# The last layer norm of an attention and expert layer begun two tiles early: rows of the last two tiles summed on chip and written over

## The reference

```python
logits = xf @ wr + br
topk_vals, topk_idx = jax.lax.top_k(logits, K)          # K = 2 of E = 4 experts
gates = jax.nn.softmax(topk_vals, axis=-1)
h = gelu(einsum('nd,edh->enh', xf, w1) + b1)            # 256 -> 1024
y = einsum('enh,ehd->end', h, w2) + b2                  # 1024 -> 256
...
out = einsum('nk,nkd->nd', gates, y_sel - c_sel + c_sum)
x = layernorm(x + out)                                  # 4096 tokens (8 x 512), 256 features
```

## Time and profile before

| | us |
|---|---|
| median of 3 runs | 1062.55 (1061.18 to 1064.93) |
| the profiled execution | 1066.83 |
| its span on the core | 1065.1 |
| PE busy | 929.2 (87%) |
| DVE busy | 835.0 (78%) |
| ACT busy | 495.6 (47%) |
| POOL busy | 430.5 (40%) |

### The profile page before, as it was taken

The page is one execution under the profiler, slowest core; times in us unless marked ns, Lnnn a source line. Parts: engine busy times, 40 slices in busy tenths (PEclk is TensorE's granted clock), DMA queues, the critical chain, the costliest instruction groups (busy, mean ns, idle before and its releaser), DMA issues.

```text
span 1065.1 us, 26698 instructions
## 1 busy us (share of the span) xinstructions
PE 929.2 (87%) x8002; PEld 676.0 (63%) x8003; DVE 835.0 (78%) x2990; ACT 495.6 (47%) x1045; POOL 430.5 (40%) x376
## 2 busy tenths in 40 slices
PE   3688999997989989998896799899999999999920
PEld 1244656555656566565664577788889778988920
DVE  4637789797898988988987789887777887777737
ACT  3256554553555635555355545343444333333304
POOL 6418055383453653735537512223222442322321
PEclk8789999999999999999999989999999999999975
DMA  4785103224133032230133432223223332232356
GB/s 141 250 213 147 32 22 105 80 70 118 35 91 92 25 120 59 62 119 2 51 111 120 159 110 41 41 52 47 46 42 61 81 59 45 50 50 50 50 124 222
DMA packets 61535, 90.33 MB, mean 85 GB/s; under 512 B 8620, under 2 KB 51136, under 8 KB 60384
## 3 DMA queue, kind: packets, MB, share of 16 engines
q1 hardware_dynamic: 45832, 62.73, 19.9%
q0 software_dynamic: 14304, 21.90, 11.2%
q10 hardware_dynamic: 1280, 4.19, 1.1%
HBM read 52.80 MB, written 35.86 MB: 83 GB/s over the span
## 4 chain that ended last, share of the span: by engine, by line
PE 55%; DVE 25%; issue 6%; DMA 6%; SPq 4%; ACT 2%; DVEq 1%; POOL 0%; ACTq 0%; POOLq 0%
PE sm L1375 6%; PE st L1375 5%; PE ms L1160 5%; PE sm L1388 5%; PE pv L1388 5%; PE sm L1242 5%; PE st L1202 4%; PE pv L1222 4%; DVE junk L1780 4%; PE ms L1300 3%; DVE arena_b L1942 3%; DVE arena_b L1940 2%; PE ms L1272 2%; DVE beaten L1727 2%; PE st L1204 2%
## 5 line engine op out<-in xcount | busy, mean ns | idle before, releaser
L1780 DVE CUSTOM_DVE_ANT_0 junk<-sm,mask_ts 128x512 bf16<-128x512 f32 (+3 forms) x512 | 220.1, 485 | 61.1 <-PE sm L1242 58.7
L900 POOL DMA_INDIRECT sums<-arena_b x70 | 112.6, 1609 | 294.7 <-DVE arena_b L1968 280.6
L1028 ACT ACTIVATE arena_b<-st 128x512 f32<-128x512 f32 x320 | 180.2, 598 | 101.6 <-PE st L1204 100.2
L1202 PE MATMUL st<-arena_a 128*128 128x384 f16 (+3 forms) x512 | 126.5, 304 | 24.1 <-ACT arena_b L1028 16.7
L1242 PE MATMUL sm<-arena_a 128*128 128x512 f16 (+3 forms) x512 | 112.9, 309 | 18.0 <-DVE maxes L1780 11.9
L1942 DVE TENSOR_TENSOR arena_b<-arena_b 128x256 f16<-128x256 f32 x280 | 120.2, 429 | 9.6
L1099 ACT ACTIVATE arena_b<-sm,arena_b 128x256 f32<-128x256 f32 x140 | 66.1, 474 | 125.5 <-PE sm L1375 107.0
L1375 PE MATMUL st<-arena_b,arena_a 128*128 128x256 f16 x840 | 115.6, 275 | 7.7 <-DVE arena_b L1659 6.9
L1940 DVE CAST arena_b<-arena_b 128x256 f16<-128x256 f32 x280 | 88.8, 317 | 38.5 <-ACT arena_b L1099 36.9
L1388 PE MATMUL pv<-arena_a,arena_b 128*128 x864 | 118.0, 275 | 0.0
L1099 ACT ACTIVATE arena_b<-st,arena_b 128x256 f32<-128x256 f32 x140 | 65.9, 473 | 111.0 <-PE st L1375 95.9
(11 more groups left out here) (292 smaller groups left out, 1675.0 us busy)
## 6 DMA issues: line engine op xcount, KB each, us to landing
arena_b<-slots SPq DMA_DIRECT2D x37, 260.0 KB, 2.8
arena_a<-w SPq DMA_DIRECT2D x8, 1024.0 KB, 6.8
arena_b<-x_tr SPq DMA_DIRECT2D x8, 512.0 KB, 4.2
q_rows<-arena_b SPq DMA_DIRECT2D x32, 128.0 KB
k_rows<-arena_b SPq DMA_DIRECT2D x32, 128.0 KB
arena_a<-q_rows SPq DMA_DIRECT2D x32, 128.0 KB
arena_a<-k_rows SPq DMA_DIRECT2D x32, 128.0 KB
res<-x_tok POOLq DMA_DIRECT2D x8, 512.0 KB, 4.7
```

The costliest lines, as they stand in the source:

```text
L900: pool.indirect_dma_start(sums, bass.IndirectOffsetOnAxis(ap=token_now[:, 1 - par, m:m + 1], axis=0), y_out[1 - par][:, m, :], None, compu ...
L1028: act.activation(probs[:, q, :], st_ps[piece % 2][:, :], ACT.Exp, scale=SCORE_SCALE).then_inc(exp_done, 1)
L1202: pe.matmul(out[:, at:at + width], ks[:, h % 2, h // 2, s * P:(s + 1) * P], qs[:, h // 2, s * P:T], start=m == 0, stop=False, skip_group_c ...
L1780: last = dve.tensor_tensor_reduce(junk[:, n % 3, at:at + width], sm_ps[n % 3][:, at:at + width], mask_ts[:, T - width:T], 1.0, NEG, ALU.ad ...
```

## The change

Two of the 35 tiles, 33 and 34, are kept apart (`KEPT` = 2). Their steps are no longer in the loop but written out after it (the loop has 10 steps in place of 12), and their results aren't added to `sums`.

- SP waits for the adds of tiles 0 to 32 only, and loads the rows of all tokens in five groups of 12, 8, 4, 4 and 4 blocks, blocks 8 to 19 first, into the free buffers. They are normalised and stored as they are. For tokens with a row in tile 33 or 34 this lacks those tiles' part.
- POOL gathers, for the 512 rows of the two tiles, their tokens' rows of `sums` into `res` (four indirect transfers of 128 rows).
- In step 34 PE spreads the 512 token numbers over all partitions (four products in single precision, in place of the turning of a next tile's rows), and DVE compares them with the token number of each row: `same` is a 512 x 512 matrix of ones and zeros, in four operations of 128x512. After the last tile PE multiplies it by the two tiles' results (`kept_sums`, sixteen products of 128x128 by 128x256 in single precision): each row gets the sum over all rows of its token. DVE adds the gathered rows (`kept_rows`), and these four blocks are normalised as a fifth group.
- After all stores have landed, POOL writes the four blocks over the rows in `out` (four indirect transfers). Rows without a token, and the second row of a token that has two, go to 512 spare rows behind the output's 4096.
- The layer norm's own arithmetic: blocks 0 to 7 get sum and sum of squares by ACT, eight and eight operations, each with an accumulated output; the others BN_STATS as before. The start value of 1/sqrt is exp(-0.5 ln(v)) on ACT (two operations), then one round of Newton and the shift on DVE (four operations in place of thirteen and one). ACT loads the table for ln and exp once. Scaling is split by `SCALED_BY`: of the 32 token blocks ACT takes 12, POOL 16 and DVE 4 (before: 24, 8 and none); of the four kept blocks ACT and DVE take two each. Stores go out in eight units of four blocks.
- On DVE the statistics of blocks 8 to 15 stand before the down half of tile 34.

```diff
-GROUPS = [(0, 8), (8, 16), (16, 24), (24, 28), (28, BLOCKS)]
+GROUPS = [(8, 16), (16, 24), (0, 8), (24, BLOCKS), (BLOCKS, BLOCKS + KEPT_BLOCKS)]
+UNITS_STORED = (2, 3, 4, 0, 5, 1, 6, 7)
+SCALED_BY = {0: "aaaa", 1: "aaaa", 2: "pppp", 3: "pppp", 4: "ppdp", 5: "ppdp", 6: "aapd", 7: "aapd", 8: "dada"}
...
-            with eng.Fori(0, (TILES - UNROLLED) // 2) as k:
+            with eng.Fori(0, (FIRST_KEPT - UNROLLED) // 2) as k:
...
+            for t in range(FIRST_KEPT, TILES):
+                tile(t, t % 2, True, True)
             tile(TILES, TILES % 2, False, True)
...
-            sp.wait_ge(added, 32 * TILES)
...
+            sp.wait_ge(added, 32 * FIRST_KEPT)
+            for n in (1, 0, 2, 3, 4):
+                first, home = homes[n]
+                sp.dma_start(home, sums_by_block[:, first:first + home.shape[1], :]).then_inc(fin_in[n], 16)
...
-                if down:
+                if down and not kept(t - 1):
...
+            pool.wait_ge(kept_set, KEPT)
+            pool.wait_ge(added, 32 * FIRST_KEPT)
+            for n in range(KEPT_BLOCKS):
+                pool.indirect_dma_start(rows_kept[:, n, 0:D], None, sums, bass.IndirectOffsetOnAxis(ap=token_kept[:, n // 2, n % 2:n % 2 + 1], axis=0)).then_inc(kept_moved, 16)
+            places_of_kept_rows()
...
+            pool.wait_ge(out_s, 16 * len(UNITS_STORED))
+            for n in range(KEPT_BLOCKS):
+                pool.indirect_dma_start(out, bass.IndirectOffsetOnAxis(ap=token_out[:, n // 2, n % 2:n % 2 + 1], axis=0), rows_kept[:, n, 0:D], None).then_inc(kept_moved, 16)
...
+            act.preload_act_table_set("natural_log_exp_and_others")
+            sums_of(SUMMED_BY_ACT)
+            seed(0)
+            squares_of(SUMMED_BY_ACT)
+            seed(1)
+            seed(2)
+            scaled(2)
+            seed(3)
+            scaled(3)
+            seed(KEPT_GROUP)
+            scaled(KEPT_GROUP)
...
+                pe.wait_ge(same_done, KEPT_BLOCKS)
+                for k in range(KEPT):
+                    pe.wait_ge(yg_done, 2 * (FIRST_KEPT + k + 1))
+                    for n in range(2):
+                        for to in range(KEPT_BLOCKS):
+                            last = pe.matmul(st_ps[to // 2][:, to % 2 * D:(to % 2 + 1) * D], same[:, 2 * k + n, to * P:(to + 1) * P], y_out[(FIRST_KEPT + k) % 2][:, n, :],
...
+                if not up:
+                    dve.wait_ge(same_done, KEPT_BLOCKS)
+                    dve.tensor_reduce(again[:, :], same[:, 2:4, 0:ROWS], AX.X, ALU.max).then_inc(same_done, 1)
+                    statistics(8, 16)
+                    aggregates(0)
                 if down:
...
             ffn_schedule(dve, tile, lambda: dve.wait_ge(table_done, 9))
...
+            deviations(0)
+            statistics(16, 24)
+            aggregates(1)
+            statistics(24, 28)
+            squares_in(2)
+            deviations(1)
+            deviations(2)
+            scaled(1)
+            statistics(28, 32)
+            aggregates(3)
+            kept_rows()
+            statistics(BLOCKS, BLOCKS + KEPT_BLOCKS)
+            deviations(3)
+            scaled(3)
+            aggregates(KEPT_GROUP)
+            deviations(KEPT_GROUP)
+            scaled(KEPT_GROUP)
```

More of the change, by code:

```diff
@@ L472, in place_of, with blocks_for, done_by @@
             return (n + C - 1) % C
[L474 to L479, removed]
+        def blocks_for(engine, g):
+            return [n for n in range(*GROUPS[g]) if SCALED_BY[n // UNIT][n % UNIT] == engine[0]]
+        def done_by(engine, blocks):
+            order = [n for g in range(len(GROUPS)) for n in blocks_for(engine, g)]
+            return max([order.index(n) + 1 for n in blocks if n in order], default=0)
         def half(t):
             return t // 2 if isinstance(t, int) else Count(t.k, t.a // 2, t.b // 2)
-        assert UNROLLED % 2 and not (TILES - UNROLLED) % 2
+        assert UNROLLED % 2 and not (FIRST_KEPT - UNROLLED) % 2 and KEPT == 2
         def ms_bank(i, n):
@@ L500, in later, with kept @@
             return (i if isinstance(i, int) else i.b) >= n
+        def kept(t):
+            return isinstance(t, int) and t >= FIRST_KEPT
         def before_end(i, n):
@@ L685, in tile @@
                         sp.wait_ge(table_done, 6)
-                    load_rows(t + 2, par)
+                    if not kept(t):
+                        load_rows(t + 2, par)
                     tail(mine, t, 0)
@@ new lines, in _ @@
+            pool.wait_ge(kept_set, KEPT)
[3 more added lines that the diff above has]
+            places_of_kept_rows()
+            for g in range(len(GROUPS)):
+                for n in blocks_for("pool", g):
+                    pool.wait_ge(fin_ready, g + 1)
+                    pool.tensor_scalar(fin(n), fin(n), rs_f[:, 1, n:n + 1], shift_f[:, n:n + 1], ALU.mult, ALU.add).then_inc(scaled_pool, 1)
@@ new lines, in _, with statistics, aggregates @@
+            seen = [0]
+            def statistics(first, end):
+                for n in range(first, end):
+                    if n >= BLOCKS:
+                        dve.wait_ge(kept_sum, (n - BLOCKS) // 2 + 1)
+                    else:
+                        dve.wait_ge(fin_in[home_of(n)], 16)
+                    dve.bn_stats(bst_f[:, n, :], fin(n)).then_inc(fin_stats, 1)
+            def aggregates(g):
+                first, end = GROUPS[g]
+                for n in range(first, end):
+                    seen[0] += 1
+                    dve.wait_ge(fin_stats, seen[0])
+                    dve.bn_aggr(mean_var_f[:, n, :], bst_f[:, n, :]).then_inc(fin_whole, 1)
+                dve.wait_ge(fin_whole, seen[0])
+                dve.tensor_scalar(rs_f[:, 0, first:end], mean_var_f[:, first:end, 1], LN_EPS, None, ALU.add).then_inc(fin_var, 1)
@@ L1970, in _, with scaled @@
+            def scaled(g):
+                for n in blocks_for("dve", g):
+                    dve.wait_ge(fin_ready, g + 1)
+                    dve.tensor_scalar(fin(n), fin(n), rs_f[:, 1, n:n + 1], shift_f[:, n:n + 1], ALU.mult, ALU.add).then_inc(scaled_dve, 1)
             dve.wait_ge(table_done, 3)
```

233 lines of the change are left out of this document (161 added, 72 removed).

## The result

| | before | after |
|---|---|---|
| median, 20 runs each on one chip, us | 1063.03 (1057.16 to 1068.66) | 1059.22 (1055.06 to 1062.59) |
| the profiled execution, us | 1066.83 | 1061.78 |
| its span, us | 1065.1 | 1060.1 |
| end of PE's last second-layer product, us | 1019.06 | 1019.25 |
| end stage: from there to the span's end, us | 46.0 | 40.85 |

The ratio is 0.9959, with a 95% interval from 0.9945 to 0.9973: 4.4 us less, between 2.9 and 5.8. The ratio itself is beyond the 0.3%, 3.2 us, that I had called measurable; the weak end of its interval is just short of it. The forecast, 5.7 us less, lies just inside the interval's other end. The time was forecast at 1056.8 us, between 1053.8 and 1062, from an earlier median of 1062.55; the median came at 1059.22, in the upper half of that range. The span was forecast at 1059.4 and came at 1060.1.

A forecast was written before the change was run, and what follows sets the result against it. PE bounds the tiles; the change acts on the 46.0 us end stage: 17.3 gained at the start, 3.3 and 8.3 lost to load-to-landing and writing over; 5.7 off the median 1062.55 gives 1056.8 us, range 1053.8 to 1062.

The forecast's parts named there:

- The start: First load of the end stage goes out once tile 32's adds land, at 1012.22 us: 17.3 us earlier.
- Loads: Blocks 8 to 19 land at 1020.9 us, blocks 0 to 7 at 1023.9, with 1.5 us charged for the gathers.
- ACT's sums: Eight accumulating sums of blocks 0 to 7 at 0.59 us each, 4.7 us, before the first group's start value.
- The rival of dearer accumulation: Accumulating ACT operations cost more than 0.59 us; at 0.8 the time is 1060.2 us; chance 0.09.
- DVE's list: DVE's statistics, deviations, scalings and additions from 1030.1 us to the shift of blocks 24 to 31: 13.2 us.
- ACT's last four: ACT's scaling of its last four blocks after DVE's last shift: 2.1 us, to 1045.4.
- the last landing: Last store after ACT's scaling: 3.3 us for 512 KB, 0.5 of queueing, 0.1 for SP, landed at 1049.3.
- The writing over: POOL's four overlapping writes after all stores: 0.7 + 3.8 + 3.8 = 8.3 us, bounds 7.4 and 12.0.
- the slower rival: The four writes over the output go one after another; at 4.5 us a landing the time is 1067.3; chance 0.08.
- and 1.8 to the end: From the last write's landing to the span's end, 1.8 us as after the last store before; span 1059.4.
- Port: Rival: DVE and POOL hinder each other, costing 2.4 us (time 1059.2) or 4.5 us (1061.3); chance 0.17.
- Cover: PE's sums for the kept rows end at 1030.0 us, 1033.5 at half clock, before DVE needs them at 1039.8.

The follow-up runs named there:

- the new order: Changed kernel with SP waiting for the writes over, start values earlier on ACT, blocks 0 to 7 as last token group: 1107.61 us, ratio 0.9957.
- The two reordered kernels: The new order (0.9957), and the same with ACT's start value of blocks 0 to 7 ahead of its scaling of blocks 24 to 31: 1103.83 us, 0.9922.

## Why the prediction was right, and where it was off

The sign, the size and the mechanism held; four terms were off. Three made the forecast too slow, by 3.6 us together, and one too fast by 4.25. That they cancel to 0.7 is luck.

- **The start**: right in kind, 18.4 us of span time earlier for the 17.3 forecast. The second add of tile 32 was issued 1.16 us sooner than before, half because DVE's result was ready sooner (1005.26 for 1005.89), half because POOL began at once (1005.27) and not 0.60 behind it; that the written-out step does this is likely and not shown. PE's end was forecast at 1019.5 and came at 1019.25.
- **Loads**: `o_t` landed at 1023.92, as forecast (1023.9), but by two errors: the start was 1.1 us early, and the gathers took 2.7 us (12.37 beside them, 9.70 without), not 1.5. `outer` landed at 1018.9, 2 us sooner than forecast; DVE took it up at once, and the chain doesn't go through it.
- **ACT's sums**: the term of 0.59 us was mis-sized. I had added the reading of the accumulator; it is overlapped, and one takes 0.40, less even than the plain operation with two operand pointers, for scale and bias (0.51). With the small ones the term is 3.9 and not 5.4 us, so DVE's first `deviations` were done at 1028.6, 1.5 sooner. The rival of dearer accumulation is out.
- **DVE's list** was 12.6 us for 13.2; ACT's last four 2.1 as forecast; the last landing 3.5 for 3.9. Together the last store landed at 1046.86 and not at 1049.3.
- **The writing over**: 7.2 us for 8.3. The four writes start 1.3 us apart, as forecast, and overlap, so the slower rival is out. Their landing takes 2.4 us, not the adds' 3.8, so that the 7.2 lie even below the 7.4 that I had given as the lower bound. (The upper bound, 12.0, comes to 11.6 by its own terms.) Here the estimate from the Trainium skill's page DMA: Bandwidth & Descriptors, section on the anatomy of a DMA, 2.3 us, was the better one, and the row of the adds was the wrong neighbour. An add has to take in the row that is there and a plain write doesn't; that this is the difference was not tested.
- **"and 1.8 to the end"** is the step that failed. I took what lay behind the last landing of before for a fixed tail. It was POOL's DRAIN, begun 4.4 us before that landing. The change puts POOL's last work behind the stores, so the tail became 6.05 us, 4.25 more than the 1.8. Kernels without the writes, with the wait on SP, and with POOL done early in the kernel before all show it. The views that I had read, chain, waits and timeline, don't list it as work; the rows of L171 and L178 do.
- **Port**: three operations of DVE's list were slower beside POOL, the two scalings with 0.50 and 0.64 us for 0.35 and one of 128x8 with 0.34 for 0.17, together 0.6 us and not 2.4 or 4.5; DVE's list as a whole was shorter than forecast. That rival is out at this size. Half of a scaling was a wrong reading of the earlier trace rows: DVE's small operation began at 1043.17, 0.13 us behind POOL's scaling, and ended at 1043.61, as that did (1043.04, 0.55 each). The one here did the same (1034.41 to 1034.75, POOL's from 1034.19). These two waited for the rest of the scaling, so their price hung on when they began.
- **Cover**: PE's sums were done at 1028.1 at full clock (forecast 1030.0, or 1033.5 at half), and DVE took them up at 1037.95. They cost nothing; nor did they in the kernel with late loads, where PE did the second half at a granted clock of 0.50.

The sum against the forecast: start -1.1, load to last landing 35.7 for 37.1, -1.4, writing over -1.1, end +4.25: +0.7, which is 1060.1 for 1059.4.

Open: what POOL does in its DRAIN, and whether it depends on the number of transfers that it has issued; no run here varies that. The early start without the new arithmetic was not run. With the arithmetic alone and with the new order the end stage is some 3 us shorter than that of the kernel before and of the changed kernel, and the times don't show it. The two reordered kernels were timed in different batches, and their difference by time, 0.9957 and 0.9922 with intervals that overlap, isn't settled.

## What to carry to other kernels

Before moving an engine's last work, look at how each engine's program closes: here POOL's ends 5.4 to 5.7 us behind its last operation at the earliest, which is nearly free beside a last store and is paid in full behind it. In this kernel partial work begun early paid one for one along the operand that landed last, so put the short operations on which others wait (a start value) ahead of long runs in an in-order list, and look for the next such run at once. For a transfer of a kind that the trace doesn't show, a row that does more (an add) is a cautious bound and not the value to take.

## What the runs showed of the hardware

- POOL's closing DRAIN lasted 5.66 us where POOL had been idle for 1.5 us before it, 5.98 where one last scaling ran at its start, 6.68 where two did, and 9.39 where three writes were still to be issued. Its end lay 5.4 us behind the end of a last scaling, 5.7 behind that of a last write, and 7.3 behind that of a last write for whose landing POOL waited first.
- An ACT operation of 128x256 with accumulated output took 0.40 us without operand pointers, and the squares, which have one pointer, 0.49. The reading of the accumulator, 0.19, ran beside the next operation.
- An indirect write of 128 rows landed in 2.4 us, with four issued 1.3 us apart; the adds of the same size needed 3.8.
- Four gathers of 128 rows, 0.52 MB, beside the loads: a load of 1 MB behind one of 1.5 MB landed in 12.37 us, in 9.70 in the kernel in which the gathers were through, and in 9.5 in the one without gathers.
- PE kept a granted clock of 1.00 (2.4 GHz) through 1.67 us of waiting and single-precision products with gaps, and until 1030, 1.9 us past its last product; it was at 0.83 in the window from 1030 to 1032 and at 0.50 (1.2 GHz) after. In the kernel with late loads it stood for 9.2 us before the second half of the sums, the granted clock fell to 0.50, and these took 6.24 us for 3.72.
